# A transformer block with 64 experts: a table of token places is read in parts while it is written, half-finished rows are made on VectorE, the shared expert's weights are scaled before use, and TensorE adds part of the last sums

## The chip, the cores and the metric

The kernel runs on one core of a Trainium2 chip. The metric is the device time of one launch in microseconds. The engines are TensorE (PE; PEld is its weight load), VectorE (DVE), ScalarE (ACT), GpSimd (POOL) and SyncE (SP). SP issues nearly all plain transfers; POOL issues the indirect ones, which scatter or gather rows by a list of indices. The engines run their instructions in written order and meet only at semaphores.

## What is computed

The input x has 4 batches of 512 tokens with 512 features, 2048 tokens in all. A small product gives six rows per batch (sa, ca, ga, sb, cb, gb). All of it is float32.

```python
h = layernorm(x) * (1 + ca) + sa
Q, K, V = split(h @ W_in.T + b_in); Q, K = rope(Q), rope(K)      # rope on the first 256 features
A = sum over tokens of (K / |K|) * V                             # one row per batch
x = x + ga * ((A * Q) @ W_out.T + b_out + h)
h2 = layernorm(x) * (1 + cb) + sb
topv, topi = top_k(h2 @ gate_w.T, 8)                             # 64 experts, 8 picks for a token
W = softmax(topv) scattered to [tokens, 64]
out = sum over e of (silu(h2 @ g_e.T) * (h2 @ u_e.T) * W[:, e]) @ dp_e.T     # inner width 128
out = out + sigmoid(h2 @ sh_gate1.T) * (silu(h2 @ sh_g.T) * (h2 @ sh_u.T)) @ sh_down.T
x = x + gb * out
```

Only the rows that picked an expert are computed for it: 16384 pairs of token and pick.

## The kernel before

**Attention stage, about 0 to 345 us.** A loop over batches b = 0 to 3, each with 4 tiles of 128 tokens. For each batch PE projects with the weighted `W_out` (`project`, L1388), makes keys and values of batch b + 1 (L1343), turns the normed rows h2 so that features lie on partitions (`turn_h2`, L1401), scores the experts (L1421), ranks the picks (L1488, L1489), makes the queries of b + 1 (L1354), and sums the keys (L1365, L1377). ACT takes the turned rows out of PSUM with scale and shift (`turned_h2`, L684); these are finished h2 values, transposed. For batches 0 to 2, PE turns them back (`turn_back`, L1410, 16 transposes a batch) and ACT copies them into `h2` (`rows_back`, L691), from where SP stores them in DRAM (`h2_rows`, L460). For batch 3, DVE instead multiplies and adds the rows `rows_b` to the normed rows (`finish_h2`, L376 and L378, 8 instructions). DVE runs the attention's elementwise work in a fixed order; within it `take_sums` (L949) feeds PE's `turn_sums` (L1377), and `weigh_w_out` (L958, L962) takes that result and makes the weights of the next `project`.

**The slot table.** For each batch, DVE computes where each of the token's 8 picks goes (`place`, L972), and POOL scatters the pair numbers to `slot_table` in DRAM with 32 indirect transfers a batch (L553), 128 in all. `key` is rank plus 2048 times the expert's number, and the maximum instruction sorts it downwards, so pick 7 of a token is its expert with the lowest number and pick 0 the one with the highest. After all have landed, SP reads the table into SBUF in 4 pieces (L481). DVE sums up how many tiles each expert has (`plan`, L1207 and L1208).

**Shared expert.** PE computes it for batch 0 in the attention stage and for batches 1 to 3 (`KEPT`, `HELD`, `LAST`) right behind it (L1461, L1477). DVE adds its output to x in two instructions for a tile of 128 tokens (`shared_sum`, L1126 and L1129): the product of PSUM, gate and `rows_g` (gb), then the sum.

**Expert stage, about 394 to 912 us.** Work goes by tiles of 128 pairs, at most 192 of them, in rounds of 8. For a tile, DVE takes the token numbers from the table (`tokens`, L1219), POOL gathers the rows from `h2_rows` (L585, 7 tiles ahead), PE turns them (L1573), multiplies with gate and up (`gate_up`, L1578), turns the product (`turn_inter`, L1593) and multiplies with down (L1586); ACT and DVE work between (L769, L775, L1228, L1242, L1236), and POOL scatters the result to `y_rows` (L595). PE runs two tiles of `turn` and one of `gate_up` ahead of `turn_inter`. SP loads an expert's weights into one of 4 slots (L467).

**Last stage, about 912 to 986 us.** Each token has 8 rows in `y_rows`. SP reads 2 of the 8 (`early`) during the last experts (L504) into 32 buffers, and the other 6 for one group of 128 tokens at a time, 5 groups ahead (`read_back`, L507, two transfers of 768 KB). For a group, PE adds 4 rows by products with the identity (L1647); DVE first adds the two early rows of all 16 groups (L1274), then for each group the last two rows (L1279), the early sum (L1281), the sum in PSUM (L1283), multiplies by `rows_g` (L1284) and adds to x (L1285). `s_fo` counts finished groups; each lets SP read another group and write one out (L536).

## Time and profile before

| | us |
|---|---|
| median of 3 runs | 988.71 (987.8 to 989.61) |
| the profiled execution | 987.97 |
| its span | 986.0 |
| PE busy | 921.3 (93%) |
| DVE busy | 544.8 (55%) |
| ACT busy | 277.2 (28%) |
| POOL busy | 467.0 (47%) |

The span runs from the first to the last recorded instruction; the execution took 1.97 us more. Busy time is a sum over stages with different limits, so it doesn't tell what one stage is worth. Names in a row are those of the program, with buffer numbers left out; several tiles are views of the large buffer `front`. A float32 product of PE appears as two records, a transpose as one.

### The profile page before, as it was taken

The page shows a single profiled execution, that of the slowest core. Times are in us where ns is not written, and L with a number is a line of the kernel's source. Part 1 is how long each engine was busy: PE and PEld are TensorE (multiplying, and loading weights), DVE is VectorE, ACT ScalarE, POOL GpSimd, SP SyncE. Part 2 cuts the span into 40 slices and gives each one's busy share as a digit, 9 for nine tenths or more (in the row PEclk, how much of TensorE's full clock was granted, in tenths as well). Part 3 has the DMA queues.
Part 4 walks back from the last instruction along what each step waited for, and adds up shares of the span by engine and source line. Part 5 has one row for each costly group of instructions (what it writes and reads, how often), then busy time and mean ns, then how long its engine had stood idle before and what let it go on. Part 6 is the DMA issues. An engine that isn't in the chain of part 4 may idle for free.

```text
span 986.0 us, 18701 instructions
## 1 busy us (share of the span) xinstructions
PE 921.3 (93%) x3617; PEld 570.6 (58%) x3618; DVE 544.8 (55%) x1454; ACT 277.2 (28%) x801; POOL 467.0 (47%) x462
## 2 busy tenths in 40 slices
PE   6999999899999793999999999999999999997697
PEld 2424534354453541677777777777777777775242
DVE  3685773775764665244444444444444444443897
ACT  2011323123221300333333333333333333332000
POOL 0000035306616675466666666666666666656000
PEclk9999999999999797899999999999999999999799
DMA  9924002011102041467766777777778776896798
GB/s 336 326 74 146 1 1 81 1 43 51 31 5 87 2 150 61 132 241 249 241 232 231 251 259 272 258 260 243 234 235 271 248 238 229 306 399 269 258 417 358
DMA packets 67366, 190.49 MB, mean 193 GB/s; under 512 B 19414, under 2 KB 20054, under 8 KB 66952
## 3 DMA queue, kind: packets, MB, share of 16 engines
q1 hardware_dynamic: 37080, 118.71, 33.9%
q0 software_dynamic: 30256, 71.43, 22.0%
q8 instruction: 12, 0.20, 0.1%
q14 instruction: 18, 0.15, 0.0%
HBM read 157.41 MB, written 52.54 MB: 213 GB/s over the span
## 4 chain that ended last, share of the span: by engine, by line
PE 70%; DVE 7%; DMA 6%; issue 4%; POOL 3%; SPq 0%; DVEq 0%; ACT 0%; POOLq 0%; ACTq 0%
PE bank L1578 26%; PE bank L1586 13%; PE bank L1343 7%; PE bank L1573 7%; PE bank L1388 6%; PE bank L1354 4%; POOL slot_table L553 3%; DMA wqkv<-in_experts 2%; DMA front<-y_rows 2%; PE bank L1593 2%; DMA front<-h_rows,gid 1%; PE bank L1365 1%; PE bank L1647 1%; PE bank L1461 1%; DMA y_rows<-front,sid 1%
## 5 line engine op out<-in xcount | busy, mean ns | idle before, releaser
L1578 PE MATMUL bank<-wqkv,h2T 128*128 x1280 | 305.8, 382 | 0.5 <-DMA wqkv<-in_experts 0.5
L553 POOL DMA_INDIRECT slot_table<-pair,place x128 | 131.1, 1025 | 251.4 <-DVE place L972 187.8
L1578 PEld LDWEIGHTS bank<-wqkv,h2T 128*128 128x128 f32 x1280 | 232.7, 192 | 26.4 <-issue 0.8
L595 POOL DMA_INDIRECT y_rows<-front,sid x160 | 163.4, 1021 | 131.5 <-issue 60.8
L585 POOL DMA_INDIRECT front<-h_rows,gid x167 | 170.7, 1022 | 63.5 <-issue 44.0
L1586 PE MATMUL bank<-wqkv,front 128*128 x320 | 164.0, 594 | 1.4 <-DVE front L1242 1.4
L769 ACT ACTIVATE h2T<-bank 128x512 f32<-128x512 f32 x162 | 96.7, 597 | 207.5 <-PE bank L1573 207.5
L1573 PEld LDWEIGHTS bank<-const,front 128*128 128x128 f32 x648 | 81.9, 143 | 105.7 <-issue 102.7
L1242 DVE COPY front<-bank 128x128 f32<-128x128 f32 x160 | 46.7, 292 | 171.6 <-PE bank L1593 169.1
L1236 DVE COPY front<-bank 128x512 f32<-128x512 f32 x160 | 110.7, 692 | 42.8 <-PE bank L1586 42.4
L1343 PE MATMUL bank<-wqkv,front 128*128 128x512 f32 x256 | 115.3, 602 | 8.7 <-DVEq L904 5.9
L1573 PE MATMUL bank<-const,front 128*128 128x128 f32 x648 | 99.4, 277 | 20.5 <-DMA front<-h_rows,gid 20.5
L1343 PEld LDWEIGHTS bank<-wqkv,front 128*128 128x128 f32 x256 | 47.9, 192 | 67.1 <-issue 58.5
L1219 DVE TENSOR_SCALAR gid<-tbl 128x1 int32 x167 | 25.7, 154 | 68.1 <-issue 68.0
L1228 DVE SCALAR_TENSOR_TENSOR front<-bank,wgt,front 128x128 f32<-128x128 f32 x160 | 56.2, 351 | 9.8 <-ACT front L775 9.0
L1388 PE MATMUL bank<-front 128*128 128x512 f32 x128 | 58.3, 608 | 2.9 <-DVE front L962 2.1
L775 ACT ACTIVATE front<-bank 128x128 f32<-128x128 f32 x160 | 44.3, 277 | 54.7 <-PE bank L1578 52.7
L1354 PE MATMUL bank<-front,wqkv 128*128 128x512 f32 x128 | 57.6, 599 | 0.0
L1586 PEld LDWEIGHTS bank<-wqkv,front 128*128 128x128 f32 x320 | 48.3, 191 | 14.3 <-issue 2.4
L784 ACT ACTIVATE wgt<-front 128x1 f32 x160 | 32.5, 203 | 83.4 <-DMA y_rows<-front,sid 42.3
L1647 PE MATMUL bank<-front,const 128*128 128x512 f32 x92 | 44.0, 630 | 10.4 <-DMA front<-y_rows 10.4
L1593 PE MATMUL bank<-const,front 128*128 128x128 f32 x160 | 43.7, 273 | 0.8 <-issue 0.8
(234 smaller groups left out, 766.8 us busy)
## 6 DMA issues: line engine op xcount, KB each, us to landing
wqkv<-in_experts SPq DMA_DIRECT2D x64, 768.0 KB
front<-y_rows SPq DMA_DIRECT2D x20, 768.0 KB, 9.7
wqkv<-y_rows SPq DMA_DIRECT2D x12, 768.0 KB, 12.4
front<-in_w_mod SPq DMA_DIRECT2D x5, 1024.0 KB, 10.3
x<-in_x SPq DMA_DIRECT2D x4, 1024.0 KB, 11.2
h_rows<-h SPq DMA_DIRECT2D x4, 1024.0 KB, 5.9
out_dram<-x SPq DMA_DIRECT2D x16, 256.0 KB, 10.3
wqkv<-in_w_in SPq DMA_DIRECT2D x3, 1024.0 KB, 13.5
```

What stands on the lines that cost most here:

```text
L553: pool.indirect_dma_start(out=slots[:, :], out_offset=bass.IndirectOffsetOnAxis(ap=place[b % 2][:, i, k:k + 1], axis=0), in_=pair[:, b * T ...
L585: pool.indirect_dma_start(out=xg[s], out_offset=None, in_=h2_rows[:, :], in_offset=bass.IndirectOffsetOnAxis(ap=gid[:, s:s + 1], axis=0), ...
L595: pool.indirect_dma_start(out=y_rows[:, :], out_offset=bass.IndirectOffsetOnAxis(ap=sid[:, s:s + 1], axis=0), in_=yb[s % YBUFS], in_offset ...
L769: sc.activation(h2T[:, s % 4, :], bank[s % 2][:, :], ACT.Copy).then_inc(s_xT, 1)
L1236: ve.tensor_copy(yb[s % YBUFS], bank[4 + s % 2][:, :]).then_inc(s_y, 1)
L1343: mm = pe.matmul(bank[2 + j][:, :], hT[:, k, i * P:(i + 1) * P], win[:, k, (j + 1) * D:(j + 2) * D], start=(k == 0), stop=(k == KC - 1))
L1354: mm = pe.matmul(bank[4 + c % 2][:, :], win[:, k, c * P:(c + 1) * P], hT[:, k, :], start=(k == 0), stop=(k == KC - 1))
L1388: mm = pe.matmul(bank[4 + i % 2][:, :], qT[:, k, i * P:(i + 1) * P], woa[:, k, :], start=(k == 0), stop=(k == KC - 1))
L1573: mm = pe.transpose(bank[s % 2][:, k * P:(k + 1) * P], xg[s][:, k * P:(k + 1) * P], ident)
L1578: mm = pe.matmul(bank[2 + s % 2][:, 0:GU], xT[s % 4][:, k, :], wqkv[:, bass.ds(w + k * GU, GU)], start=(k == 0), stop=(k == KC - 1))
L1586: pe.matmul(bank[4 + s % 2][:, :], iT[s % 2], wqkv[:, bass.ds(w + KC * GU, D)], start=True, stop=True).then_inc(s_d, 1)
L1593: pe.transpose(bank[6 + s % 2][:, 0:P], inter[s % 2], ident).then_inc(s_I, 1)
```

## The change

**Rows of h2.** `turn_back` and `rows_back` are gone. `finish_h2` now runs on DVE for every batch: two tiles between `take_sums` and `weigh_w_out`, two behind it. SP loads `rows_b` for each batch.

**Scaled down weights.** DVE multiplies the shared down weights by `rows_g` once for each batch (`scale_down`) into spare buffers, and `shared_sum` becomes one instruction a tile instead of two.

**The table in parts.** POOL scatters the last batch's picks in the order 7, 6, 5, then 4, 3, then 2, 1, then 0. When those of one kind have landed, SP reads the part of the table that they complete: experts 1 to 3, 4 and 5, 6 and 7, and at the end the other 57 in three pieces. Tiles 0 to 2 can only be of experts 1 to 3, and so on, so DVE takes their tokens and POOL gathers their rows between the scatters. DVE's first round waits for all parts. PE starts on the first tiles without waiting for the last shared sums.

**Early rows.** For groups 0 to 7, PE adds the two early rows by products with the identity, into 8 banks, ahead of all groups; DVE adds them only for groups 8 to 15.

```diff
+PICKS = [(7, 6, 5), (4, 3), (2, 1), (0,)]
+PARTS = [(1, 4), (4, 6), (6, 8), (8, 27), (27, 46), (46, EXPERTS + 1)]
+PART_OF_TILE = [0, 0, 0, 1, 1, 2, 2, 5]
...
+down_w = [region[5][:, 3 * D:4 * D]]
...
+down_w += [r[:, 2 * i:2 * i + 2, :].rearrange("p a c -> p (a c)") for r, i in ((kcos, 0), (kcos, 1), (ksin, 0))]
...
-down_banks = {0: (2, 3, 2, 3), KEPT: (2, 3, 6, 7), HELD: (4, 5, 2, 3), LAST: (0, 1, 6, 7)}
+down_banks = {0: (2, 3, 2, 3), KEPT: (2, 3, 6, 7), HELD: (4, 5, 2, 3), LAST: (6, 7, 4, 5)}
...
-def finish_h2(eng):
-
-    eng.wait_ge(s_rows_b, 32)
-    eng.wait_ge(s_tpC, KC * BATCH)
-    for i in range(TPB):
+def finish_h2(eng, b, tiles=range(TPB)):
+
+    eng.wait_ge(s_rows_b, 32 * (b + 1))
+    eng.wait_ge(s_tpC, KC * (b + 1))
+    for i in tiles:
         eng.tensor_tensor(h2[:, i, :], h2[:, i, :], rows_b[:, 0, :], ALU.mult).then_inc(s_h2m, 1)
-        eng.wait_ge(s_h2m, i + 1)
+        eng.wait_ge(s_h2m, TPB * b + i + 1)
         eng.tensor_tensor(h2[:, i, :], h2[:, i, :], rows_b[:, 1, :], ALU.add).then_inc(s_h2, 1)
 
...
-    load_rows_b(LAST)
+    load_rows_b(0)
...
+        if b + 1 < BATCH:
+            load_rows_b(b + 1)
...
-    for e in range(1, WSLOTS + 1):
-        if e > 1:
-            sp.wait_ge(s_w, 16 * (e - 1))
-        load_w(e)
-
-
+    def load_table(i):
+        a, b = PARTS[i]
+        sp.dma_start(tbl[:, a * SLOT_COLS:b * SLOT_COLS],
+                     slots[:, :].rearrange("(p c) w -> p (c w)", p=P)[:, (a - 1) * SLOT_COLS:(b - 1) * SLOT_COLS]).then_inc(s_tbl[i], 16)
+
+    def picks_in(i):
+        sp.wait_ge(s_scat_last[i], 16 * TPB * len(PICKS[i]))
+
+    load_w(1)
     sp.wait_ge(s_scat[0], 16 * TOPK * TPB * 2)
     sp.wait_ge(s_scat[1], 16 * TOPK * TPB)
-    for done in s_scat_last:
-        sp.wait_ge(done, 16 * TOPK * TPB // 2)
-    for i in range(4):
-        n = EXPERTS * SLOT_COLS // 4
-        sp.dma_start(tbl[:, SLOT_COLS + i * n:SLOT_COLS + (i + 1) * n],
-                     slots[:, :].rearrange("(p c) w -> p (c w)", p=P)[:, i * n:(i + 1) * n]).then_inc(s_tbl[i], 16)
+    picks_in(0)
+    load_table(0)
+    sp.wait_ge(s_w, 16)
+    load_w(2)
+    sp.wait_ge(s_w, 32)
+    load_w(3)
+    picks_in(1)
+    load_table(1)
+    sp.wait_ge(s_w, 48)
+    load_w(4)
+    picks_in(2)
+    load_table(2)
+    picks_in(3)
+    for i in range(3, len(PARTS)):
+        load_table(i)
...
+    def scatter_picks(i, tiles):
+
+        for k in PICKS[i]:
+            for n in tiles:
+                put_pair(LAST, n, k, s_scat_last[i])
...
-    for n in range(0, TOPK * TPB, 4):
-        if n >= 8:
-            pool.wait_ge(s_scat_last[n // 4 % 2], 64 * (n // 8))
-        scatter(LAST, n, n + 4)
-    pool.wait_ge(s_tbl[0], 16)
-    pool.wait_ge(s_plan, 2)
-    pool.wait_ge(s_h2w, 16 * BATCH)
-    pool.wait_ge(s_ww, 16 * BATCH)
-    pool.wait_ge(s_o, TPB * BATCH)
-    pool.wait_ge(s_shg, KEPT + 1)
+    pool.wait_ge(s_place, LAST + 1)
+    scatter_picks(0, range(HT))
+    pool.wait_ge(s_place, LAST + 2)
+    scatter_picks(0, range(HT, TPB))
+    scatter_picks(1, range(TPB))
 
...
-    for n in range(AHEAD):
-        pool.wait_ge(s_gid, n + 1)
-        gather(n, n)
+    pool.wait_ge(s_plan, 2)
+    pool.wait_ge(s_h2w, 16 * BATCH)
+    pool.wait_ge(s_ww, 16 * BATCH)
+    pool.wait_ge(s_o, TPB * BATCH)
+    pool.wait_ge(s_shg, KEPT + 1)
+
+    def first_gathers(tiles):
+        for n in tiles:
+            pool.wait_ge(s_gid, n + 1)
+            gather(n, n)
+
+    first_gathers(range(0, 3))
+    pool.wait_ge(s_scat_last[0], 16 * TPB * len(PICKS[0]))
+    scatter_picks(2, range(TPB))
+    first_gathers(range(3, 5))
+    pool.wait_ge(s_scat_last[1], 16 * TPB * len(PICKS[1]))
+    scatter_picks(3, range(TPB))
+    first_gathers(range(5, AHEAD))
...
-    def rows_back(b):
-        sc.wait_ge(s_tpC, KC * (b + 1))
-        for i in range(TPB):
-            sc.wait_ge(s_back, TPB * b + i + 1)
-            sc.activation(h2[:, i, :], bank[i % 2][:, :], ACT.Copy).then_inc(s_h2, 1)
...
-            key_norms(b + 1, range(2, 3))
-            rows_back(b)
-            key_norms(b + 1, range(3, TPB))
+            key_norms(b + 1, range(2, TPB))
...
+    def scale_down(b):
+        ve.wait_ge(s_rows_g, 16 * BATCH)
+        ve.wait_ge(s_shw, 16)
+        ve.tensor_tensor(down_w[b], shared_w[:, KC * GU:WROW], rows_g[:, b, :], ALU.mult).then_inc(s_dw, 1)
+
     def shared_sum(b, tiles=range(TPB)):
 
-        ve.wait_ge(s_rows_g, 16 * BATCH)
         for i in tiles:
             g = b * TPB + i
             ve.wait_ge(s_shd, g + 1)
-            if g:
-                ve.wait_ge(s_shx, g)
-            ve.scalar_tensor_tensor(out=shared_out, in0=bank[down_banks[b][i]][:, :], scalar=gate_sh[:, g:g + 1],
-                                    in1=rows_g[:, b, :], op0=ALU.mult, op1=ALU.mult).then_inc(s_sht, 1)
-            ve.wait_ge(s_sht, g + 1)
-            ve.tensor_tensor(x_at(g), x_at(g), shared_out, ALU.add).then_inc(s_shx, 1)
+            ve.scalar_tensor_tensor(out=x_at(g), in0=bank[down_banks[b][i]][:, :], scalar=gate_sh[:, g:g + 1],
+                                    in1=x_at(g), op0=ALU.mult, op1=ALU.add).then_inc(s_sht, 1)
...
+    def first_tokens(tiles):
+        for n in tiles:
+            ve.wait_ge(s_tbl[PART_OF_TILE[n]], 16)
+            tokens(n, n)
...
             take_sums(b + 1)
+            finish_h2(ve, b, range(0, HT))
             weigh_w_out(b + 1)
+            finish_h2(ve, b, range(HT, TPB))
             if b == 0:
                 shared_inner(0)
+                scale_down(0)
         else:
...
+            scale_down(1)
             add_x(b, 0, tb)
+            scale_down(2)
             add_x(b, 1, tb)
             roots2_half(b, 0, tb)
             add_x(b, 2, tb)
             add_x(b, 3, tb)
             roots2_half(b, 1, tb)
+            scale_down(3)
             for j in range(2):
                 choose_half(b, j, tc)
...
+            ve.wait_ge(s_plan, 2)
+            first_tokens(range(0, 3))
             shared_inner(HELD)
             shared_sum(KEPT)
+            first_tokens(range(3, 5))
             shared_inner(LAST)
             shared_sum(HELD)
-
...
+            shared_sum(LAST)
+            first_tokens(range(5, AHEAD))
+            ve.wait_ge(s_sht, TILES)
...
-    shared_sum(BATCH - 1)
-    ve.wait_ge(s_plan, 2)
-    ve.wait_ge(s_tbl[0], 16)
-    for n in range(AHEAD):
-        tokens(n, n)
-    for i in range(1, 4):
+    for i in range(3, len(PARTS)):
...
-    for g in range(TILES):
+    for g in range(BANKS, TILES):
         ve.tensor_tensor(early[0][g], early[0][g], early[1][g], ALU.add).then_inc(s_esum, 1)
     tf = Tally(s_fm)
     for g in range(TILES):
         part = back[g % BACK]
         ve.wait_ge(s_fl[g % BACK][1], 16 * (g // BACK + 1))
         step(tf, ve.tensor_tensor(part[4], part[4], part[5], ALU.add))
-        ve.wait_ge(s_esum, g + 1)
-        step(tf, ve.tensor_tensor(part[4], part[4], early[0][g], ALU.add))
+        if g >= BANKS:
+            ve.wait_ge(s_esum, g - BANKS + 1)
+            step(tf, ve.tensor_tensor(part[4], part[4], early[0][g], ALU.add))
         ve.wait_ge(s_ft, g + 1)
-        step(tf, ve.tensor_tensor(part[4], part[4], bank[g % BACK][:, :], ALU.add))
+        step(tf, ve.tensor_tensor(part[4], part[4], bank[g % BANKS][:, :], ALU.add))
         step(tf, ve.tensor_tensor(part[4], part[4], rows_g[:, g // TPB, :], ALU.mult))
...
-    def turn_back(b, tiles):
-        for i in tiles:
-            pe.wait_ge(s_h2T, KC * (b + 1))
-            if i >= 2:
-                pe.wait_ge(s_h2, TPB * b + i - 1)
-            for c in range(KC):
-                mm = pe.transpose(bank[i % 2][:, c * P:(c + 1) * P], h2T[:, c, i * P:(i + 1) * P], ident)
-            mm.then_inc(s_back, 1)
...
+        pe.wait_ge(s_dw, b + 1)
...
-            turn_back(b, range(0, 2))
             keys_values(b + 1, (3, 1))
-            turn_back(b, range(2, TPB))
...
+            if not again and s == 0:
+                pe.wait_ge(s_sht, TPB * (HELD + 1))
             gate_up(t, s, w[s])
             w[s + 1], loaded[s + 1] = expert_of(t + 1)
+            if not again and s == 1:
+                pe.wait_ge(s_sht, TILES)
             if again or t >= 1:
...
-    pe.wait_ge(s_shx, TILES)
+    pe.wait_ge(s_shi, BATCH)
...
+    for k in range(EARLY):
+        pe.wait_ge(s_early[k], 16 * TILES)
+    pe.wait_ge(s_xT, end + 2)
+    pe.wait_ge(s_y, end)
+    apart(pe)
+    for g in range(BANKS):
+        for k in range(EARLY):
+            pe.matmul(bank[g][:, :], ident, early[k][g], start=(k == 0), stop=False)
     for g in range(TILES):
-        if g >= BACK:
-            pe.wait_ge(s_fo, g - BACK + 1)
+        if g >= BANKS:
+            pe.wait_ge(s_fo, g - BANKS + 1)
         for k in range(BY_PE):
             if k % (LATE // 2) == 0:
                 pe.wait_ge(s_fl[g % BACK][k // (LATE // 2)], 16 * (g // BACK + 1))
-            mm = pe.matmul(bank[g % BACK][:, :], ident, back[g % BACK][k], start=(k == 0), stop=(k == BY_PE - 1))
+            mm = pe.matmul(bank[g % BANKS][:, :], ident, back[g % BACK][k], start=(g >= BANKS and k == 0), stop=(k == BY_PE - 1))
```

On PE, in the attention stage behind the ranks of a batch: L1343 makes keys and values, L1410 turns rows back, L1354 makes queries. First before, then now.

```order
L1488 MATMUL bank<-mask,tri_bf 128x65
L1489 MATMUL bank<-seen,ones_bf 128x65
L1410 MATMUL bank<-const,h2T 128x128 x8
L1343 MATMUL bank<-wqkv,front 128x512 x4
L1410 MATMUL bank<-const,h2T 128x128 x8
L1354 MATMUL bank<-front,wqkv 128x512 x8
```

```order
L1526 MATMUL bank<-mask,tri_bf 128x65
L1527 MATMUL bank<-seen,ones_bf 128x65
L1387 MATMUL bank<-wqkv,front 128x512 x4
L1398 MATMUL bank<-front,wqkv 128x512 x8
L1409 MATMUL bank<-front,krn 1x512 x4
```

The 16 transposes of a batch are gone from the row, and the queries follow the keys directly.

On POOL, from the last table entries to the first results: `slot_table` rows are scatters, `front` rows are gathers. First before, then now.

```order
L544 IOTA first_row 128x64
L553 DMA slot_table<-pair,place 131072x1 x128
L585 DMA front<-h_rows,gid 128x576 x9
L595 DMA y_rows<-front,sid 16384x512
L585 DMA front<-h_rows,gid 128x576
```

```order
L567 DMA slot_table<-pair,place 131072x1 x116
L605 DMA front<-h_rows,gid 128x576 x3
L567 DMA slot_table<-pair,place 131072x1 x8
L605 DMA front<-h_rows,gid 128x576 x2
L567 DMA slot_table<-pair,place 131072x1 x4
L605 DMA front<-h_rows,gid 128x576 x4
L615 DMA y_rows<-front,sid 16384x512
```

Five gathers now stand ahead of the last scatters, three ahead of the last 12 and two more ahead of the last 4.

On PE, from the last expert tile into the last stage. First before, then now.

```order
L1586 MATMUL bank<-wqkv,front 128x512
L1647 MATMUL bank<-front,const 128x512 x11
L1647 MATMUL bank<-wqkv,const 128x512
L1647 MATMUL bank<-front,const 128x512 x3
L1647 MATMUL bank<-wqkv,const 128x512 x5
```

```order
L1622 MATMUL bank<-wqkv,front 128x512
L1683 REGISTER_ALU
L1688 MATMUL bank<-wo,const 128x512
L1688 MATMUL bank<-rows_b,const 128x512
L1688 MATMUL bank<-wo,const 128x512
L1688 MATMUL bank<-bias_kv,const 128x512
L1688 MATMUL bank<-wo,const 128x512
L1688 MATMUL bank<-bias_kv,const 128x512
```

These are the first six of sixteen products (two for each of groups 0 to 7) that now stand between the last `down` and the four of group 0 (L1695).

## Rows read from the trace of the kernel before

**Rows 1.** Stages: us, busy time of PE, PEld, DVE, ACT, POOL; granted clock, DMA share, GB/s

```profile
380.00:400.00 20.00, 3.21 (x13) 2.45 (x14) 6.35 (x16) 1.19 (x2) 10.93 (x11) 0.58 0.33 94
440.00:600.00 160.00, 160.00 (x766) 120.01 (x765) 74.41 (x205) 59.30 (x204) 104.92 (x103) 1.00 0.73 245
```

**Rows 2.** Chain that ended last, batch 2: start, length, what

```profile
288.71 0.91 PE bank L1410 x8
```

**Rows 3.** DVE in order of time, batch 2: start, length, what, idle before

```profile
308.97 0.16 DVE L958 COPY asum<-bank 128x4 f32<-128x4 f32 x1 [2.88 <-PE bank L1377]
...
317.30 0.69 DVE L1020 TENSOR_TENSOR x<-bank,x 128x512 f32<-128x512 f32 x1 [5.40 <-PE bank L1388]
```

**Rows 4.** DVE in order of time, batch 3, the rows of h2

```profile
345.15 0.69 DVE L376 TENSOR_TENSOR h<-h,rows_b 128x512 f32<-128x512 f32 x1
...
350.47 0.22 DVE L1002 SCALAR_TENSOR_TENSOR wtok<-etop,mask 128x64 f32<-128x64 f32 x1
```

**Rows 5.** PE in order of time, keys and values of batches 2 and 3

```profile
183.77 12.23 PE L1343 MATMUL bank<-wqkv,front 128*128 128x512 f32 x24 [2.84 <-issue]
...
213.84 3.70 PE L1343 MATMUL bank<-wqkv,front 128*128 128x512 f32 x8 [2.20 <-DVEq L904]
...
257.18 10.46 PE L1343 MATMUL bank<-wqkv,front 128*128 128x512 f32 x24
```

**Rows 6.** DVE in order of time, last shared sum of batch 0

```profile
183.71 0.69 DVE L1129 TENSOR_TENSOR x<-x,front 128x512 f32<-128x512 f32 x1
```

**Rows 7.** POOL in order of time, batches 2 and 3 and first gather

```profile
292.35 0.96 POOL L553 DMA_INDIRECT slot_table<-pair,place  x1 [19.06 <-DVE place L972]
...
318.32 0.96 POOL L553 DMA_INDIRECT slot_table<-pair,place  x1 [3.73 <-DMA slot_table<-pair,place]
...
341.84 1.06 POOL L553 DMA_INDIRECT slot_table<-pair,place  x1 [1.48 <-DMA slot_table<-pair,place]
...
349.63 1.03 POOL L553 DMA_INDIRECT slot_table<-pair,place  x1 [0.30 <-issue]
...
378.78 1.28 POOL L553 DMA_INDIRECT slot_table<-pair,place  x1 [0.30 <-issue]
...
383.55 1.27 POOL L553 DMA_INDIRECT slot_table<-pair,place  x1 [0.30 <-issue]
391.03 1.04 POOL L585 DMA_INDIRECT front<-h_rows,gid  x1 [6.21 <-DVE gid L1219]
```

**Rows 8.** Chain that ended last, from the last scatter

```profile
383.55 2.45 DMA slot_table<-pair,place
...
386.08 2.34 DMA tbl<-slot_table
```

**Rows 9.** PE in order of time, `turn_inter` of the second tile

```profile
407.86 0.27 PE L1593 MATMUL bank<-const,front 128*128 128x128 f32 x1
```

**Rows 10.** DVE in order of time, first tokens

```profile
389.88 0.15 DVE L1219 TENSOR_SCALAR gid<-tbl 128x1 int32 x1 [4.31 <-issue]
```

**Rows 11.** Chain that ended last, last stage

```profile
919.99 6.57 PE bank L1647 x8
...
963.83 13.70 DMA front<-y_rows
...
977.66 3.69 PE bank L1647 x8
```

**Rows 12.** DVE in order of time, start of the last stage

```profile
911.23 0.69 DVE L1236 COPY front<-bank 128x512 f32<-128x512 f32 x1 [0.70 <-PE bank L1586]
...
926.65 0.69 DVE L1283 TENSOR_TENSOR front<-front,bank 128x512 f32<-128x512 f32 x1 [3.77 <-PE bank L1647]
```

**Rows 13.** Last stage by windows, columns as in rows 1

```profile
905.00:912.00 7.00, 4.03 (x11) 1.27 (x9) 2.97 (x7) 0.50 (x3) 4.70 (x5) 1.00 0.15 51
...
920.00:924.00 4.00, 4.00 (x5) 1.84 (x6) 2.85 (x5) 0.00 (x0) 0.00 (x0) 0.50 1.02 420
...
945.00:950.00 5.00, 5.00 (x14) 2.13 (x13) 4.83 (x8) 0.00 (x0) 0.00 (x0) 1.00 1.03 426
```

51 lines of the change are left out of this document (27 added, 24 removed).

## The prediction

> **What bounds the kernel now.** I read the windows by stage first. From 440 to 600 us PE is busy 160.00 of 160 us at clock 1.00, so the expert stage is PE's, and the change leaves its instructions alone. From 380 to 400 us PE has 3.21 us of work in 20 [rows 1]. Next came the chain of waits, to see what PE lacks there. POOL's 32 scatters of batch 3 start at 341.84 us and the last at 383.55; the landing (2.45 us) and the table's read (2.34 us) end at 388.42, the first token numbers come at 389.88, the first gather at 391.03, and the second tile's `turn_inter`, from which on PE runs without a gap, at 407.86 [rows 7 to 10]. POOL is late because it has 128 scatters in a row: those of batch 2 began at 292.35, after a wait of 19.06 us for DVE's places, and the next batch follows them without a wait for DVE [rows 7]. So what counts ahead of the experts is when the places of batch 2 are known, and then POOL's own row. In the attention stage the chain is nearly all PE's. In the last stage the DMA engines run at a share of 1.03 and 426 GB/s [rows 13]: the last read is issued at 963.83 and lands after 13.70 us [rows 11].
>
> **Attention stage.** `turn_back` is six pieces of eight transposes, 0.91 us each [rows 2], on the chain: 1.8 us a batch, 5.4 in all. In their place DVE gets eight instructions a batch. In batch 3 the same eight run from 345.15 to 350.47, 5.32 us, so half is 2.66 [rows 4]. The first half stands where DVE waits 2.88 us for PE, the second where it waits 5.40 [rows 3]. Both are covered; the first with 0.2 us to spare, so an uncovered half would cost up to 2.66 a batch. ACT only loses work, which I count as nothing.
>
> In batch 1, PE stands 2.84 us before the keys of batch 2 and then needs 12.23 us for 24 records that elsewhere take 10.46 [rows 5]. It waits for the sums of the shared expert, and DVE's second instructions for them, 0.69 us each, lie in that row [rows 6]. Three of them stood ahead of the awaited one and go; one `scale_down` of the same size comes in: 1.4 us less backlog. Part of that DVE now spends waiting for PE, so I take 0.7 (bounds 0 and 1.4). The rest of the stall is then about 2 us. A stall of 2.20 us left the next eight records at 3.70 [rows 5], the full rate, so I take back the 1.8 us too (bounds 0 and 1.8). Places of batch 2 then come 1.8 + 0.7 + 1.8 + 1.8 = 6.1 us sooner, and PE's chain ends 7.9 sooner (batch 2's own `turn_back` lies behind its places).
>
> **POOL's row and the table.** Batch 2's scatters take 49.5 us to the start of batch 3's, with waits for landings in them, one of 3.73 us [rows 7]. The h2 store and the reload of kept rows now fall close together beside that wait, for which I give back 0.8 us. Batch 3's first scatter: 341.84 - 5.3 = 336.5. The 31 steps to the last took 41.71 us; undisturbed a step is 0.96 + 0.30, or 39.2 in all, and the late ones took 1.28 + 0.30 beside the shared sums [rows 7]. There are fewer of these sums now; I take 40.5 (bounds 39.2 and 41.7). Five gathers stand in between, 1.3 us each with the gap [rows 7]: 6.5. The last scatter starts at 336.5 + 40.5 + 6.5 = 383.5, as before, and the whole table is there at 388.4.
>
> The Trainium skill has a rule for this place (SBUF — State Buffer, Who interferes with whom): a VectorE instruction with at most one SBUF input, outside the two-port modes, leaves GpSimd alone. The old second sum had two such inputs, the new one has one beside PSUM. By it all steps are 1.26, and the last scatter comes 1.3 us sooner than I say. The trace agrees only in part: beside `finish_h2`, also with two SBUF inputs, a scatter took 1.03 us, not 1.28 [rows 7].
>
> The gain is in what is done by then. The picks 7, 6 and 5 are out after 12 steps (351.7), their part can be in SBUF by 357, ahead of POOL's first gather at 336.5 + 20 x 1.27 = 361.9. The small reads I price like the old ones, 2.34 us [rows 8], bounds 1 and 5; a delay below 2 us costs nothing, as the gathers wait for POOL. DVE takes three tokens ahead of the next shared product, so PE's shared work ends near 373 rather than 371; nothing needs PE then. PE does `turn` of four tiles and `gate_up` of two before DVE may enter its round. DVE enters at 388.4, and its first token costs 1.46 us (388.42 to 389.88, [rows 8, 10]), so the first `turn_inter` is at about 390.5. The second follows after one tile of PE work without `down`: a tile is 3.1 us (160 us over 51 tiles, 15 records each, [rows 1]), less 0.9 for `down`, and 2.8 more because PE has stood for some 5 us and starts at the lower clock; eight records took 6.57 us at 919.99 and 3.69 at full clock [rows 11, 13]. That is 395.5, against 407.86: **12.4 us sooner**, 5.3 of them from the attention stage. Expert tiles, weights and gathers follow PE's pace and move along.
>
> **Last stage.** DVE loses 8 sums ahead of the groups and one in each of 8 groups, over 10 us of work. I count it at nothing, since DVE was not what ended last. PE gets 16 float32 products, 32 records of 0.43 us (10.46 over 24, [rows 5]): 13.8 us. It starts when DVE has copied the last result, at 911.92 [rows 12], so it goes on at full clock (1.00 from 905 to 912, [rows 13]) and ends at 925.8; group 0's four products end at 929.3. Before, they started when the rows came, at 919.99, at 1.2 GHz (0.50, [rows 13]), and ended at 926.56 [rows 11]. So DVE's L1283 comes at 929.4 instead of 926.65 [rows 12], and with it the first finished group and the first new read. From there a group is seven pieces of 128 x 512 float32 (six read, one written), 1.84 MB, at 426 GB/s 4.3 us, while PE needs 3.45 and DVE at most 3.6: DMA is the bound, and its end moves with its start. **2.75 us later.** Bounds: 0, if the first group doesn't hold the reads, and 5.6, if 2.8 us of the added products run at half clock.
>
> **Sum.** 987.97 - 12.4 + 2.75 = 978.3 for the profiled execution, which lies 0.74 us below the median of the runs, 988.71. I predict 979.0. What a measurement of this kernel can tell from no change is 0.2%, 2 us.
>
> **Rivals.**
> - *The rows of h2 aren't covered.* The first half lies between `take_sums` and `weigh_w_out`, with 0.2 us to spare; if DVE comes to it late by the batch's other work, PE waits 2.66 us in batches 0 and 1 ahead of batch 2's places. Against it: DVE has 2.88 us idle there. 979.0 + 5.3 = 984.3. Chance 0.10.
> - *The early products are free.* If DMA has slack elsewhere in the stage, so that the later first read is made up for, the 2.75 go: 976.3. For it: DVE's load is lighter; against it, the share of 1.03. Chance 0.12.
> - *The tiles in front don't help (slower).* From the whole table to the second `turn_inter` is 19.4 us now. If the entry into the first round still takes that long, because DVE and ACT in written order keep PE from using its early tiles, the five gathers just eat up POOL's lead: the table is there at 388.4, the stage starts at 407.9, and the last stage's 2.75 us are left: 991.5. It decides if that stretch stays above some 17 us. Against it: between first token (389.88) and second `turn_inter` (407.86) lie gathers, landings and first products, which need only the first parts. Chance 0.05.
> - *The change does less than it says:* the parts come too late for the gathers ahead (DVE's tokens wait for part 0 beyond 362, as weights share the queue), each us late shifting all of POOL's row. With 4 us, 983. Chance 0.08.
>
> **How the numbers follow.** My forecast has 0.65, with its own range 973.5 to 984: 0.8 either way for the scatters, 2.5 for batch 1, 2.8 for the last stage, 1.5 for the clock at the start. The other cases, within 976 and 984.5 but for the slower one, widen it to 973 to 986.5, which leaves out the slower rival and combinations at the edges. Faster by over 0.2% 0.92, within 0.2% 0.03, slower 0.05.
>
> **What would show it.** No idle of PE before the keys of batch 2 above 2 us, and 10.4 us for their 24 records; VectorE's sum copy (now L981), four h2 instructions and L958 with no more than the old pause between them; batch 3's first scatter near 336.5, and 48 us to the last; PE idle for 5 us ahead of the first `turn_inter` near 390.5; 32 records ahead of group 0, its end some 17.5 us after the last `down`'s copy; DMA share near 1.0 to the end. It is wrong if the start of round 0 lies less than 9 or more than 15 us sooner, or the last stage is shorter than before.

## The result: 0.4% faster where 1% was forecast

The changed kernel took 984.39 us (median of 15 runs, 981.42 to 986.37), the kernel before beside it on the same chip 988.05 (15 runs, 983.75 to 991.23): ratio 0.996, 95% interval 0.9944 to 0.9975. The direction was right and the time lies in the range, but 3.7 us were gained where 9.7 were forecast. (The interval leaves room for 2.5 to 5.5 us.) The profiled execution took 985.78 us with a span of 984.0, against 987.97 and 986.0. The stages below are read from these two executions, so they add up to the 2.0 us between the two spans, not to the 3.7 between the medians.

### The profile after

The page of the changed kernel, busy time per engine and the chain by line:

```profile
span 984.0 us, 18635 instructions
PE 930.2 (95%) x3601; PEld 570.6 (58%) x3602; DVE 540.8 (55%) x1450; ACT 270.3 (27%) x789; POOL 465.4 (47%) x462
PE 69%; DMA 7%; POOL 6%; issue 5%; DVE 4%; SPq 0%; DVEq 0%; POOLq 0%
```

Totals tell little here, so I go by stage. PE in order of time in the attention stage, behind the pauses where `rank` waits for DVE's masks and at the keys of batch 2; these rows answer to [rows 5]:

```profile
127.60 5.37 PE L1387 MATMUL bank<-wqkv,front 128*128 128x512 f32 x8 [2.17 <-DVEq L936]
183.65 10.54 PE L1387 MATMUL bank<-wqkv,front 128*128 128x512 f32 x24 [2.05 <-issue]
212.01 5.40 PE L1387 MATMUL bank<-wqkv,front 128*128 128x512 f32 x8 [2.20 <-DVEq L936]
283.29 3.70 PE L1387 MATMUL bank<-wqkv,front 128*128 128x512 f32 x8 [1.86 <-DVEq L936]
```

The 24 records at 183.65 have the full rate again, as forecast, and the stall ahead of them is 0.8 us shorter. But behind the pauses of batches 0 and 1 eight records now take 5.4 us, partly at half clock (granted 0.50 from 127.6 to 130 us), where the kernel before took 3.70 (in batch 1, [rows 5]): 1.7 us lost twice, nearly the 1.8 us that `turn_back` gave in each of those batches.

POOL in order of time, from the places of batch 2 to the end of the table; answers to [rows 7]:

```profile
290.87 0.96 POOL L567 DMA_INDIRECT slot_table<-pair,place  x1 [19.67 <-DVE place L1004]
...
302.68 1.67 POOL L567 DMA_INDIRECT slot_table<-pair,place  x1 [1.46 <-DMA slot_table<-pair,place]
...
308.54 1.62 POOL L567 DMA_INDIRECT slot_table<-pair,place  x1 [0.30 <-issue]
...
319.52 0.95 POOL L567 DMA_INDIRECT slot_table<-pair,place  x1 [5.45 <-DMA slot_table<-pair,place]
...
330.77 0.96 POOL L567 DMA_INDIRECT slot_table<-pair,place  x1 [1.46 <-DMA slot_table<-pair,place]
...
343.41 0.96 POOL L567 DMA_INDIRECT slot_table<-pair,place  x1 [2.84 <-DMA slot_table<-pair,place]
...
389.53 0.96 POOL L567 DMA_INDIRECT slot_table<-pair,place  x1 [0.31 <-issue]
390.79 1.04 POOL L605 DMA_INDIRECT front<-h_rows,gid  x1 [0.30 <-issue]
```

The first scatter of batch 3 (343.41) is 1.6 us later than before, though batch 2's began 1.5 us sooner: four waits for landings stand between, 11.2 us together, where the kernel before has 9.1 (1.46, 3.73, 2.45 and 1.48). The scatters themselves, with their gaps, take 1.0 us more than before: the two at 302.68 and 308.54, beside `finish_h2`, took 1.67 and 1.62 us. The last scatter is 6.0 us later than before.

The chain of waits from there (answers to [rows 8]), and PE's entry into the expert stage (answers to [rows 9]):

```profile
389.53 2.21 DMA slot_table<-pair,place
...
392.60 4.19 DMA tbl<-slot_table
```

```profile
387.17 1.90 PE L1614 MATMUL bank<-wqkv,h2T 128*128 x8
398.23 0.45 PE L1629 MATMUL bank<-const,front 128*128 128x128 f32 x1 [9.16 <-DVE front L1277]
...
402.74 0.42 PE L1629 MATMUL bank<-const,front 128*128 128x128 f32 x1
```

PE has done two tiles' first products and then stands 9.16 us until the table is whole. The second `turn_inter` comes 5.1 us sooner than before, where 12.4 were forecast. The expert stage behind it loses none of this: to the end of the last copy it takes 502.5 us (504.1 before).

The first half of `finish_h2` ends 0.2 us before `take_sums`' result is there, and behind the second half DVE still waits for PE (DVE in order of time, batch 2; answers to [rows 3]):

```profile
305.79 0.16 DVE L990 COPY asum<-bank 128x4 f32<-128x4 f32 x1 [0.22 <-PE bank L1421]
...
314.12 0.69 DVE L1052 TENSOR_TENSOR x<-bank,x 128x512 f32<-128x512 f32 x1 [2.14 <-PE bank L1432]
```

The last stage, PE in order of time and two windows (columns as in [rows 1]):

```profile
905.30 1.53 PE L1688 MATMUL bank<-wo,const 128*128 128x512 f32 x2 [0.83 <-issue]
...
920.81 9.60 PE L1695 MATMUL bank<-front,const 128*128 128x512 f32 x22
```

```profile
905.00:910.00 5.00, 4.70 (x7) 2.03 (x8) 5.00 (x10) 0.00 (x0) 1.90 (x2) 0.66 0.18 26
...
920.00:925.00 5.00, 5.00 (x13) 2.23 (x12) 0.49 (x1) 0.00 (x0) 0.00 (x0) 1.00 0.02 3
```

The added products run from 905.30 to 920.81, group 0's behind them. DVE waits 13.9 us for it, nothing frees a buffer, and the DMA engines stand still from 920 to 925 us (share 0.02). From the last copy's end (905.20) to the end are 78.8 us, 4.7 more than the 74.1 before.

### The profile page after: what moved, and what is told of

Its sections match the earlier page's. It is cut to its first block, busy times and chain, and to the rows that moved or that the text cites. A ratio compares the mean times of both kernels' runs of the same rounds, so it can differ in the third digit from the quotient of the medians.

```text
span 984.0 us, 18635 instructions
## 1 busy us (share of the span) xinstructions
PE 930.2 (95%) x3601; PEld 570.6 (58%) x3602; DVE 540.8 (55%) x1450; ACT 270.3 (27%) x789; POOL 465.4 (47%) x462
## 4 chain that ended last, share of the span: by engine, by line
PE 69%; DMA 7%; POOL 6%; issue 5%; DVE 4%; SPq 0%; DVEq 0%; POOLq 0%
PE bank L1614 26%; PE bank L1622 13%; PE bank L1387 7%; PE bank L1609 6%; POOL slot_table L567 5%; PE bank L1432 4%; PE bank L1695 3%; PE bank L1398 3%; DMA wqkv<-in_experts 2%; PE bank L1629 2%; PE bank L1688 2%; DMA front<-y_rows 1%; DMA slot_table<-pair,place 1%; PE bank L1409 1%; PE bank L1496 1%
## 5 line engine op out<-in xcount | busy, mean ns | idle before, releaser
L802 ACT ACTIVATE front<-bank 128x128 f32<-128x128 f32 x160 | 44.1, 276 | 53.6 <-PE bank L1614 52.5
L1432 PEld LDWEIGHTS bank<-front 128*128 128x128 f32 x128 | 24.4, 194 | 33.0 <-issue 31.2
```

The source lines that it names most:

```text
L1432: mm = pe.matmul(bank[4 + i % 2][:, :], qT[:, k, i * P:(i + 1) * P], woa[:, k, :], start=(k == 0), stop=(k == KC - 1))
```

## The experiments

Each kernel has one profiled execution, with these places in it (us). "Pauses": time of the eight records behind the pause in batches 0, 1, 2. "Keys": the 24 records near 183 us. Then the first scatter of batches 2 and 3, the last scatter, the second `turn_inter`, and the last stage (last copy's end to end of span). Each kernel was timed beside the kernel before on the same chip, e5 to e8 on another chip than the other experiments, so across the table the ratios compare, not the medians. A place in the table is that of one execution; e8 shows how far two executions of one program can lie apart.

| kernel | pauses | keys | scatter b2 | scatter b3 | last | turn_inter 2 | last stage | median of runs | ratio to before (95%) |
|---|---|---|---|---|---|---|---|---|---|
| before | 3.70 3.70 3.70 | 12.23 | 292.35 | 341.84 | 383.55 | 407.86 | 74.1 | 988.05 | 1 |
| changed | 5.37 5.40 3.70 | 10.54 | 290.87 | 343.41 | 389.53 | 402.74 | 78.8 | 984.39 | 0.996 (0.9944 to 0.9975) |
| e1 | 3.67 3.67 3.67 | 12.23 | 289.71 | 341.36 | 387.68 | 401.02 | 78.7 | 982.98 | 0.9959 (0.9934 to 0.9984) |
| e2 | 5.40 3.70 3.70 | 10.54 | 289.86 | 341.58 | 387.71 | 399.88 | 74.5 | 980.32 | 0.9927 (0.9903 to 0.995) |
| e3 | 5.40 3.70 3.70 | 10.54 | 289.52 | 341.81 | 388.14 | 401.25 | 72.5 | 977.75 | 0.9913 (0.9881 to 0.9946) |
| e4 | 5.40 5.40 3.70 | 10.54 | 291.24 | 344.02 | 383.63 | 399.83 | 77.2 | 982.01 | 0.995 (0.9925 to 0.9975) |
| e5 | 5.40 5.40 3.70 | 10.54 | 291.01 | 342.61 | 388.81 | 390.76 | 79.1 | 978.14 | 0.9884 (0.9851 to 0.9917) |
| e6 | 5.40 5.40 3.70 | 10.54 | 290.82 | 342.55 | 388.86 | 400.42 | 79.4 | 982.82 | 0.9935 (0.9913 to 0.9957) |
| e7 | 5.32 5.40 5.40 | 10.54 | 292.16 | 336.48 | 382.98 | 396.09 | 78.6 | 977.0 | 0.9876 (0.9846 to 0.9907) |
| e8 | 5.31 5.40 3.70 | 12.17 | 295.42 | 344.94 | 386.79 | 408.74 | 73.8 | 987.57 | one run |
| e9 | 5.40 3.70 3.70 | 12.23 | 294.94 | 344.87 | 391.14 | 404.52 | 79.8 | 986.63 | 0.998 (0.9954 to 1.0005) |
| e10 | 5.40 5.40 3.70 | 10.54 | 290.73 | 335.05 | 381.23 | 383.13 | 72.1 | 963.31 | 0.976 (0.9732 to 0.9788) |
| e11 | 3.67 3.67 3.67 | 10.54 | 287.82 | 332.13 | 378.27 | 379.97 | 73.0 | 961.19 | 0.9733 (0.9705 to 0.9761) |

### e1: the pauses filled

```diff
+def warm(b):
+    for n in range(16):
+        pe.transpose(bank[0][:, n % KC * P:(n % KC + 1) * P], h2T[:, n % KC, 0:P], ident)
-keys_values(b + 1, (2, 1), (3, 0))
+keys_values(b + 1, (2, 1))
+warm(b)
+keys_values(b + 1, (3, 0))
```

> The changed kernel with 16 transposes (into a free bank, results unused) put into TensorE's pause of about 2.2 us ahead of the last keys of the next batch, in batches 0, 1 and 2. Theory (the clock took back what turn_back gave): TensorE's clock fell to 1.2 GHz behind these pauses in batches 0 and 1 (5.37 and 5.40 us for eight records that take 3.70 at full clock). With the pause filled the eight records take 3.70 us in both, the queries of batches 1 and 2 start 1.7 us sooner each, and the whole is 1.5 to 3.4 us faster than the changed kernel (985.8 profiled gives 982.4 to 984.3). Rival (the pause is not what made the clock fall; it fell by chance or by what lay before, as the kernel before had the same pause at the same place and kept 3.70): at least one of the two stays at 5.4 us, and the time is that of the changed kernel within 1 us.

Behind the filled pauses all three stretches kept the full rate. PE in order of time:

```profile
128.04 3.67 PE L1387 MATMUL bank<-wqkv,front 128*128 128x512 f32 x8 [0.51 <-DVEq L936]
182.36 12.23 PE L1387 MATMUL bank<-wqkv,front 128*128 128x512 f32 x24 [2.05 <-issue]
212.50 3.67 PE L1387 MATMUL bank<-wqkv,front 128*128 128x512 f32 x8 [0.54 <-DVEq L936]
```

But the clock now fell behind the next unfilled stall, that of 2.05 us at the keys of batch 2 (granted 0.61 from 182.3 to 186 us), and took 1.7 us there. Batch 2's first scatter is 1.2 us sooner than in the changed kernel. The time (982.98) can't be told from the changed kernel's: the intervals overlap almost wholly. So the clock's part is right as a mechanism and wrong as a sum: of the 3.4 us filled at the pauses, 1.7 were lost at the keys. Whether the filling moved the loss there is not shown: e9, with its pauses unfilled, has the same 12.23 us behind the same stall, and eight other executions with that stall have 10.54.

### e8: the kernel before once more

> The kernel before, profiled once more. Theory (where TensorE's clock falls behind a pause of some 2 us is fixed by the schedule): again 3.70 us for the eight records behind the pauses near 127 and 213 us, and 12.23 us for the 24 keys records near 184 us. Rival (it differs from execution to execution): at least one of the three is different, as 5.4 or 10.5 us.

The rival held. The same program, PE in order of time:

```profile
127.19 5.31 PE L1343 MATMUL bank<-wqkv,front 128*128 128x512 f32 x8 [2.16 <-DVEq L904]
185.21 12.17 PE L1343 MATMUL bank<-wqkv,front 128*128 128x512 f32 x24 [2.84 <-issue]
215.21 5.40 PE L1343 MATMUL bank<-wqkv,front 128*128 128x512 f32 x8 [2.21 <-DVEq L904]
287.84 3.70 PE L1343 MATMUL bank<-wqkv,front 128*128 128x512 f32 x8 [1.50 <-DVEq L904]
```

With slow records behind the pauses in batches 0 and 1, as the changed kernel has, batch 2's first scatter comes at 295.42. The execution of before on which I predicted was a lucky one at that place: no slow stretch behind any pause, 292.35. Compared like with like, the change brings the places of batch 2 4.5 us sooner (295.42 to 290.87), not 1.5. Little of e8's lateness reached its expert stage: from the last scatter to the second `turn_inter` it took 22.0 us, the first execution 24.3, so that `turn_inter` is 0.9 us later (408.74) and the time the same (987.57). Against e8 the changed kernel's second `turn_inter` is 6.0 us sooner, not 5.1: the luck of one execution at one place can be undone at the next.

### e9: the first part alone undone

`turn_back` and ACT's copies again, `finish_h2` and SP's loads of `rows_b` for batch 3 only; the rest as in the changed kernel.

```diff
+turn_back(b, range(0, 2))
 keys_values(b + 1, (3, 1))
+turn_back(b, range(2, TPB))
...
-finish_h2(ve, b, range(0, HT))
 weigh_w_out(b + 1)
-finish_h2(ve, b, range(HT, TPB))
```

> The changed kernel with its first part alone undone: the h2 rows of batches 0 to 2 come back from TensorE's transposes (turn_back) and ACT's copies, as before; the scaled down weights, the table in parts and the early products stay. Theory (turn_back's time was a gain of about 4.5 us for TensorE ahead of batch 2's places, of which POOL lost some 2.5 again, because the stores and reloads then meet its landing waits): batch 2's first scatter starts 3 to 5 us later than the 290.87 of the changed kernel, its scatters take 49.5 to 50 us instead of 52, and the last batch's first scatter comes 1 to 2 us later than there, 343 to 345.5; the time is 0 to 3 us above the changed kernel. Rival (all of the part's gain reaches the end): last batch's first scatter 4.5 us later, time 4 to 5 us above the changed kernel.

The theory held: batch 2 starts 4.1 us later (294.94) and its scatters take 49.9 us, so batch 3 starts only 1.5 us later. Both executions have two slow stretches, at different places. SyncE's queue shows what moved, first of e9, then of the changed kernel:

```profile
296.88 0.36 SPq L467 DMA_DIRECT2D h_rows<-h  x1
301.85 0.36 SPq L469 DMA_DIRECT2D h_rows<-wtok  x1
314.83 0.33 SPq L463 DMA_DIRECT2D front<-h2t_kept  x1
```

```profile
311.41 0.37 SPq L466 DMA_DIRECT2D h_rows<-h  x1
311.82 0.51 SPq L468 DMA_DIRECT2D h_rows<-wtok  x1
312.37 2.42 SPq L424 DMA_DIRECT2D rows_b<-mod_rows  x2
314.89 0.44 SPq L462 DMA_DIRECT2D front<-h2t_kept  x1
```

With the h2 rows finished late, behind `weigh_w_out`, the store of 1 MB, the row loads and the reload of 1 MB go out within 4 us, while POOL waits for its second eight scatters (5.45 us against 3.77). Which of these transfers makes the wait longer is not shown; the four waits together are 11.2 us against 9.4 in e9. The scatters of that group, two of which took 1.67 and 1.62 us beside `finish_h2` in the changed kernel, took at most 1.20 here. In time e9 is 0.2% above the changed kernel, with overlapping intervals.

### e7: landings waited for one group later

For batch 2 only; its last landings are waited for in the middle of batch 3's first picks.

```diff
-scatter(b, n, n + TOPK)
-landed(b, n + TOPK)
+if b < LAST - 1:
+    scatter(b, n, n + TOPK)
+    landed(b, n + TOPK)
+    continue
+if n >= 2 * TOPK:
+    pool.wait_ge(s_mid[n // TOPK % 2], 16 * TOPK * (n // (2 * TOPK)))
+pool.wait_ge(s_place, b + 1)
+for k in range(TOPK):
+    put_pair(b, n // TOPK, k, s_mid[n // TOPK % 2])
...
+for done in s_mid:
+    pool.wait_ge(done, 16 * TOPK * TPB // 2)
 scatter_picks(0, range(HT, TPB))
```

> The changed kernel, but in batch 2 POOL waits for the landings of the eight scatters before the last eight, not for those of the last eight, with two semaphores in turn. Theory (landing waits in POOL's row, 1.46 + 5.45 + 1.46 + 2.84 us in the changed kernel, made the first scatter of the last batch start at 343.41 instead of 336.5): POOL has its batch-2 scatters out by 332 and then waits for VectorE's places of the last batch, which come near 339 to 341.5; its first scatter starts 2 to 4 us sooner and so does everything to the first turn_inter: time 2 to 4 us below the changed kernel. Rival (the transfers themselves stand in a row, so that a later wait waits as long): the first scatter stays at 341.4 to 344 and the time within 1 us.

POOL, first scatter of batch 3:

```profile
336.48 0.95 POOL L570 DMA_INDIRECT slot_table<-pair,place  x1 [2.18 <-DVE place L1016]
```

From the first scatter of batch 2 to the first of batch 3 are now 44.3 us, though batch 2 began at 292.16 (behind three slow stretches). Batch 3 starts at 336.48, 6.9 us sooner than in the changed kernel, and waits for VectorE's places instead. I had expected 2 to 4: I had put those places at 339 to 341.5, and the first half is there at 336.5. The time is 977.0, ratio 0.9876, clear of the changed kernel's interval. So the landing waits, not VectorE, held batch 3.

### e4: the gathers behind the scatters

```diff
-first_gathers(range(0, 3))
 pool.wait_ge(s_scat_last[0], 16 * TPB * len(PICKS[0]))
 scatter_picks(2, range(TPB))
-first_gathers(range(3, 5))
 pool.wait_ge(s_scat_last[1], 16 * TPB * len(PICKS[1]))
 scatter_picks(3, range(TPB))
-first_gathers(range(5, AHEAD))
+first_gathers(range(AHEAD))
```

> The changed kernel with POOL's five gathers that stand between the scatters of the last batch moved behind all of them. Theory (POOL's row sets when the table is whole, and the whole table gates VectorE's round 0): the last scatter starts 6.7 us sooner, near 382.8 instead of 389.53, and the table is whole near 389.5 instead of 396.8. The gathers come near 384 to 391 instead of 369 to 392, so PE's first turn lies near 389; the second turn_inter comes at about 397.5, 5 us sooner than the 402.74 of the changed kernel. Rival (tiles in front pay, as the change has it): TensorE then lacks tiles, the second turn_inter comes at 402.7 or later, up to 407.9, and the time is the same or up to 5 us worse.

The last scatter came 5.9 us sooner, though batch 3 had begun 0.6 later: five gathers cost 6.5 us there, as the prediction had it. The second `turn_inter` came at 399.83, 2.9 us sooner than in the changed kernel, not 5: now PE waits for the gathers. PE in order of time:

```profile
388.61 1.09 PE L1607 MATMUL bank<-const,front 128*128 128x128 f32 x4 [7.07 <-DMA front<-h_rows,gid]
391.01 2.06 PE L1607 MATMUL bank<-const,front 128*128 128x128 f32 x8 [1.32 <-DMA front<-h_rows,gid]
```

So the tiles in front are worth nothing as long as something else waits for the whole table; taking them away was no loss (982.01, not to be told from the changed kernel).

### e6: two gathers behind the table

```diff
+for i in range(3, len(PARTS)):
+    pool.wait_ge(s_tbl[i], 16)
 first_gathers(range(5, AHEAD))
```

> The changed kernel, but POOL's gathers of tiles 5 and 6 wait until the table is whole. Theory (the table's last read takes 4.19 us instead of 2.34 because these two gathers, 0.5 MB, move in the same microseconds): the read takes 2.3 to 2.7 us and the first turn_inter comes 1.5 to 1.9 us sooner after the last scatter (6.8 to 7.2 us after it instead of 8.7). Rival (the read is slower by its form, three pieces of 152 KB from SP instead of four of 128 KB): it stays near 4.2 us and nothing moves.

```profile
388.86 2.27 DMA slot_table<-pair,place
...
391.99 2.48 DMA tbl<-slot_table
```

The table's read takes 2.48 us instead of 4.19 (the chain of waits), and the first `turn_inter` lies 7.05 us behind the last scatter, not 8.70. The theory held.

### e5: VectorE doesn't wait for the whole table

```diff
-for i in range(3, len(PARTS)):
-    ve.wait_ge(s_tbl[i], 16)
 round_ve(0)
...
-tokens(t + AHEAD, (s + AHEAD) % ROUND)
+if not isinstance(r, int) or s > WAITED:        # WAITED = 3
+    tokens(t + AHEAD, (s + AHEAD) % ROUND)
+elif s == WAITED:
+    for i in range(3, len(PARTS)):
+        ve.wait_ge(s_tbl[i], 16)
+    for n in range(WAITED + 1):
+        tokens(n + AHEAD, (n + AHEAD) % ROUND)
```

> The changed kernel, but VectorE does not wait for the whole table before its first round: the products and copies of the first three tiles come first, and the wait for the table's last parts with the tokens of tiles 7 to 10 stands ahead of the fourth. Theory (the tiles in front give nothing because VectorE, not TensorE or the gathers, waits for the whole table): PE's idle of 9.1 us ahead of the first turn_inter (398.23 with the last scatter at 389.53) goes down to 1 to 2 us; the first turn_inter lies near 389, the second near 391, and three tiles (some 9 us of TensorE) are done when the table is whole; some 2 to 4 us are lost again to tile 7, whose gather still needs the whole table. The time is 5 to 9 us below the changed kernel, 975 to 979. Rival (the gathers of tiles 3 to 6, or POOL's row, hold the first tiles as well): the second turn_inter stays later than 397, and the gain is below 3 us.

PE in order of time:

```profile
388.23 0.30 PE L1634 MATMUL bank<-const,front 128*128 128x128 f32 x1
...
390.76 0.27 PE L1634 MATMUL bank<-const,front 128*128 128x128 f32 x1
...
400.04 0.33 PE L1634 MATMUL bank<-const,front 128*128 128x128 f32 x1 [1.67 <-DVE front L1278]
```

The 9.16 us of idle are gone. The second `turn_inter` lies at 390.76; later PE waits 0.95 us for a gather, 1.67 for VectorE (four tokens in a row behind the table) and 1.28 for a later gather. The time is 978.14 us, ratio 0.9884: its interval lies below the changed kernel's. The tiles in front pay once VectorE takes them.

### e2 and e3: the early products undone, and for three groups only

e2 sets the number of groups to 0 and goes round five banks again; e3 sets it to 3:

```diff
+BY_TENSOR = 3
-for g in range(BANKS, TILES):
+for g in range(BY_TENSOR, TILES):
     ve.tensor_tensor(early[0][g], early[0][g], early[1][g], ALU.add)
...
-for g in range(BANKS):
+for g in range(BY_TENSOR):
     for k in range(EARLY):
         pe.matmul(bank[g][:, :], ident, early[k][g], start=(k == 0), stop=False)
```

> The changed kernel with the last stage as it was: no early rows added by TensorE, VectorE sums all 16 pairs and five banks go round. Theory (the 16 added products hold group 0 back, DMA being the bound from there): from the last result's copy to the end takes 74.1 us again, not 78.8, and the time is 4.7 us below the changed kernel (about 981 profiled). Rival (something else in the changed kernel slows the last stage, such as where the rows lie or what transfers are still out): it stays near 78.8 and the time within 1 us of the changed kernel.

> The changed kernel, but TensorE adds the early rows of three groups only (6 of the 16 products); VectorE sums the other 13 pairs. Theory: six products, the first at half clock, take about 7.5 us and end when the rows of group 0 are there (8.07 us after the last copy in the kernel before), so nothing is held back, and as TensorE is then already at its higher clock group 0's own four products take 3.5 us, not 6.57. Last copy to end: 74.1 - 3.0 = 71 us, 7.7 below the changed kernel; about 978 profiled. Rival (the products' number does not matter, as the end is set by VectorE's or DMA's total): 78.8 as in the changed kernel, or no better than 74.1.

PE in the last stage, first of e2, then of e3:

```profile
908.87 12.43 PE L1691 MATMUL bank<-front,const 128*128 128x512 f32 x22 [8.80 <-DMA front<-y_rows]
```

```profile
909.34 1.02 PE L1689 MATMUL bank<-bias_kv,const 128*128 128x512 f32 x2
911.13 9.71 PE L1696 MATMUL bank<-front,const 128*128 128x512 f32 x22 [0.76 <-DMA front<-y_rows]
```

e2's last stage takes 74.5 us, the 4.3 us are back. e3's takes 72.5: its six products end 0.76 us before group 0's rows are there, and with the clock up by then (granted 1.00 from 910 to 915 us, 0.56 in e2) 22 records take 9.71 us instead of 12.43. I had expected 71. In time e2 has 0.9927 and e3 0.9913, against 0.996: e3's interval barely touches the changed kernel's and e2's overlaps it slightly, so for both the stage's own length is the better witness.

### e10 and e11: together

e10 has e3, e7 and e5 together, with e5's late tokens two at a time from the fourth tile on; e11 also fills the three pauses and the stall at the keys of batch 2:

```diff
+first = min(2 * (s - WAITED), s)
+for n in range(first, min(first + 2, s + 1)):
+    tokens(n + AHEAD, (n + AHEAD) % ROUND)
...
+if b == 1:
+    pe.wait_ge(s_hT, KC * (b + 2))
+    warm(b)
 keys_values(b + 1, (0, 0), (0, 1), (1, 0))
```

> The changed kernel with three changes together: early rows of three groups only by TensorE; VectorE's first round in the order that does not wait for the whole table, with its late tokens two at a time from the fourth tile on; landings of batch 2 waited for one group of eight later. Theory (the three losses lie on one chain and lie apart): last batch's first scatter near 336.5, second turn_inter near 384 to 386, the wait for the whole table at the fourth tile nearly covered (table whole near 390), last copy near 886 to 890, last stage 72.5 us: 960 to 964. Rival (the earlier start only meets a later limit, the gathers of tiles 5 to 8 or the weights' loads): second turn_inter as early, but idle of TensorE behind it, and 968 to 971.

> The same with transposes also in TensorE's pauses: 16 in each of the three of some 2 us ahead of the last keys, and 16 in the wait for the shared sums ahead of the keys of batch 2. Theory (each pause costs 1.7 us of half clock behind it in most executions, and filled ones none): 3.67 us behind all three pauses and 10.5 us for the 24 records near 180 us; batch 2's first scatter 1.7 to 3.4 us sooner than in the kernel without them; but POOL's first scatter of the last batch follows VectorE's places now, so it comes 1.5 to 3.4 us sooner too, and the time is 1.5 to 3.4 us lower. Rival (the clock then falls at another pause, as it did in the first filled run at the keys of batch 2): one stretch stays slow and the time is the same within 1 us.

PE of e10 at the entry into the expert stage; the only waits above 0.5 us are for gathers:

```profile
378.36 0.66 PE L1629 MATMUL bank<-const,front 128*128 128x128 f32 x4 [0.61 <-DMA front<-h_rows,gid]
...
385.39 0.66 PE L1629 MATMUL bank<-const,front 128*128 128x128 f32 x4 [1.13 <-DMA front<-h_rows,gid]
...
393.76 0.65 PE L1629 MATMUL bank<-const,front 128*128 128x128 f32 x4 [1.77 <-DMA front<-h_rows,gid]
```

e10 takes 963.31 us, 2.4% less than before (ratio 0.976, 0.9732 to 0.9788) and some 20 us less than the changed kernel. The ratios of the single experiments lay 0.0047 (e3), 0.0084 (e7) and 0.0076 (e5) below the changed kernel's 0.996, 0.0207 in sum; e10 lies 0.020 below: they add up. e11 takes 961.19 (0.9733, 0.9705 to 0.9761). Its attention stage is faster, as all four stretches have the full rate and the first scatter of batch 3 is 2.9 us sooner; of this 1.9 reach the last copy, and PE waits 2.69 us for the first rows of the last stage. The intervals of e10 and e11 overlap, so the step between them is shown in the trace, not in the time.

## Why the prediction was wrong, step by step

The forecast gave 12.4 us sooner at the second `turn_inter` and 2.75 later in the last stage, 978.3 us for the profiled execution. Measured were 5.1 and 4.7; another 1.6 came from the expert stage (e8 has 1.0 of them too, without the change), and the execution took 985.78. The step that failed most is "Batch 3's first scatter: 336.5": it was at 343.41. The terms of the sum name the right mechanisms; the clock behind the pauses, the landing waits and the read of the whole table were sized from rows that did not hold for the changed kernel, and the cost of `finish_h2` to POOL was left out.

- **turn_back's 1.8 us a batch.** The transposes went off the path, and both halves of `finish_h2` were covered (DVE still waits 0.22 and 2.14 us for PE in batch 2), so the first rival falls. What failed was the base. The sum was made against one execution in which no pause had cost a slow stretch; the changed kernel's had two, 3.4 us, and so had e8's of before. The prediction took the 3.70 behind a pause of 2.20 us as a property of the pause.
- **The stall in batch 1 and its clock.** 10.54 us for the 24 records: right. The stall became 0.8 us shorter (0.7 forecast), but it also began 0.67 us later than before, so the keys start 0.12 us sooner; that is part of the same miss. Batch 2's places came at 290.87, where 286.2 was forecast: 3.4 us of the 4.6 are the two slow stretches. Of the other 1.2, some 0.4 is the pause of batch 2, 1.86 us instead of 1.50; the rest is spread over small waits that I did not follow up.
- **"Batch 3's first scatter: 336.5."** It came at 343.41: 4.6 us from the places, and 2.3 from batch 2's scatters, which took 52.5 us where I had allowed 50.3. I gave 0.8 us to transfers meeting the landing waits; against the 49.5 of before and of e8 (and 49.9 of e9) the scatters took 3.0 us more, 2.1 of them in the waits (11.2 instead of 9.1) and 1.0 in longer scatters. e7, which takes the waits out, starts batch 3 at 336.48; that is the forecast time by another way, and no support for the sum.
- **From there to the last scatter, 47.0.** It took 46.1: right. The five gathers took 6.6 us. (31 steps of 1.26 us are 39.1, not 39.2.) All scatters beside the new shared sums took 0.95 or 0.96 us, none 1.28: so the rule of the Trainium skill that I had held at arm's length (SBUF — State Buffer, Who interferes with whom) was borne out; by it I would have said 45.7. The slow scatters beside `finish_h2`, whose instructions have two inputs in SBUF, fit it too.
- **Table 4.9 us behind the last scatter.** It took 7.3 us: 1.7 us from the two gathers that run beside the read (4.19 us against e6's 2.48), and 0.8 because the rest is read by three transfers issued in turn and VectorE waits for the last, while before its first token waited for the first only. The prediction had carried over a time that was not that of the whole table.
- **Entry into round 0, 7.1 us from the table.** It took 5.9. Sum: 6.9 - 0.9 + 2.4 - 1.2 = 7.2 us later than forecast, which is 402.74 against 395.5.
- **Last stage, +2.75.** Mechanism right, DMA being the bound from group 0 on; size 4.7. The products took 15.5 us instead of 13.8 (32 records at 10.46 over 24 would be 13.9), since TensorE's clock was at 0.66 from 905 to 910 us, not at 1.00; the bound of 5.6 had this case. L1328, the first use of group 0's sum, came 19.3 us behind the last copy instead of 14.7, 4.6 us later, and the end moved with it. The rival that the products are free is excluded by e2.
- **The slower rival** (the tiles in front don't help) had the right mechanism and too high a price: VectorE's order did keep PE from its early tiles for 9.16 us, e4 shows that they are then worth nothing, and e5 that the order was the reason. It was not decisive because the stretch from the whole table to the second `turn_inter` was 5.9 us, not 19.4.

Not settled: why one execution has a slow stretch behind a pause and another none, most of the 1.2 us in the attention stage, and which of the transfers makes POOL's landing waits longer.

## What to carry to other kernels

Before a gain in front of a queue is counted, add up the waits inside the queue and ask what the change does to them: batch 2's places came 4.5 us sooner than in e8, batch 3's first scatter 1.5. Waiting for the group before the last one took most of the 11.2 us of landing waits out and gave back more than the whole change. Work prepared early pays only if every engine that uses it waits for its own part; here one wait for the whole table in VectorE's program order was worth 6 to 8 us. And a sum made against one profiled execution inherits its luck: profile the kernel before twice where the terms are of the size of one slow stretch.
